# Half-position scans on one Trainium2 core: state products summed by accumulated 128x128 transposes and one transpose back, in place of identity products

## The reference

```
def step(h, inp):                       # at each of 1024 positions
    dA = jnp.exp(dtt[..., None] * A)    # 16 states a channel
    h = h * dA + (dtt * ut)[..., None] * bt[:, :, None, :]
    y = jnp.einsum('bkdn,bkn->bkd', h, ct)   # sum over the 16 states
    return (h, y)
```

## Time and profile before

| | |
|---|---|
| median of 3 runs | 6273.03 us |
| profiled execution, its own time | 6277.88 us |
| its span | 6276.1 us |
| PE (matmul) busy | 5337.5 us, 85% |
| DVE busy | 4868.2 us, 78% |
| POOL busy | 4099.8 us, 65% |
| ACT busy | 3324.5 us, 53% |
| mean granted TensorE clock | 0.937 of 2.4 GHz |

### The profile page before, as it was taken

One profiled execution on the slowest core, in us unless ns is written; L12 is line 12 of the kernel. 1 busy time (PEld: TensorE's weight loads), 2 busy tenths in 40 slices (PEclk: granted clock), 3 DMA queues, 4 the chain that ended last, 5 costly groups with the idle time before them and its releaser, 6 DMA issues. The chain is left out here.

```text
span 6276.1 us, 59374 instructions
## 1 busy us (share of the span) xinstructions
PE 5337.5 (85%) x16384; PEld 3080.8 (49%) x16384; DVE 4868.2 (78%) x5344; ACT 3324.5 (53%) x5102; POOL 4099.8 (65%) x3001
## 2 busy tenths in 40 slices
PE   6776777779999978878999988887999997888899
PEld 2222242246566544435566545443556563454777
DVE  7999769848888858866888876884888886787544
ACT  3433434347676646535667654662766674564221
POOL 6999538728788718845888853881888882685221
PEclk8989888889999989998999999998999998999999
DMA  5555224336667506525777733651776760562110
GB/s 194 211 209 209 76 105 165 114 110 234 238 239 243 189 25 227 203 82 175 242 250 237 250 107 115 214 172 44 250 249 228 256 219 31 191 214 102 53 46 33
DMA packets 339294, 1059.06 MB, mean 169 GB/s; under 512 B 31330, under 2 KB 121442, under 8 KB 333832
## 3 DMA queue, kind: packets, MB, share of 16 engines
q1 hardware_dynamic: 338952, 1055.17, 48.4%
HBM read 1046.13 MB, written 8.91 MB: 168 GB/s over the span
## 5 line engine op out<-in xcount | busy, mean ns | idle before, releaser
L849 PE MATMUL banks<-prod,ident 128*128 128x512 f32 x2640 | 1415.6, 635 | 446.7 <-DVE prod L1046 337.5
L987 POOL TENSOR_TENSOR h<-half_du_a,Bb 128x512 f32<-128x512 f32 x768 | 973.6, 1284 | 110.3 <-DMA Bb<-half_rows 57.1
L849 PEld LDWEIGHTS banks<-prod,ident 128*128 128x128 f32 x2640 | 475.4, 195 | 1041.9 <-DVE prod L1046 667.9
L933 ACT ACTIVATE banks<-half_delta_a,A 128x512 f32<-128x512 f32 x1152 | 765.4, 685 | 362.3 <-DVE prod L1046 188.7
L1033 DVE TENSOR_TENSOR_SCAN banks<-banks,h 128x512 f32<-128x512 f32 x660 | 807.4, 1223 | 134.0 <-POOL h L987 79.0
L996 POOL TENSOR_TENSOR h<-h,half_C_a 128x512 f32<-128x512 f32 x360 | 460.7, 1280 | 278.2 <-DVE half_carry_a L1038 178.0
L849 PE MATMUL banks<-h,ident 128*128 128x512 f32 x1200 | 639.3, 615 | 0.0
L1046 DVE TENSOR_TENSOR prod<-banks,half_C_a 128x512 f32<-128x512 f32 x792 | 548.1, 692 | 114.6 <-DMA half_C_a<-half_rows 16.2
L403 PE MATMUL banks<-prod,ident 128*128 128x512 f32 x648 | 375.3, 720 | 197.5 <-DVE prod L545 151.6
L873 PE MATMUL banks<-Cb,w_a 128*128 128x256 f32 x2304 | 533.8, 381 | 0.0
L1033 DVE TENSOR_TENSOR_SCAN banks<-banks,half_carry_a,h 128x512 f32<-128x512 f32 x396 | 506.3, 1279 | 32.4 <-ACT banks L933 23.8
(11 more groups left out here) (325 smaller groups left out, 10268.2 us busy)
## 6 DMA issues: line engine op xcount, KB each, us to landing
Bb<-half_rows SPq DMA_DIRECT2D x640, 512.0 KB, 4.2
Cb<-half_rows SPq DMA_DIRECT2D x320, 512.0 KB, 4.3
w_a<-w_in SPq DMA_DIRECT2D x256, 576.0 KB, 5.2
half_C_a<-half_rows SPq DMA_DIRECT2D x160, 512.0 KB, 7.3
w_b<-w_in SPq DMA_DIRECT2D x128, 576.0 KB, 5.2
Bb<-rows SPq DMA_DIRECT2D x96, 512.0 KB, 4.3
Cb<-rows SPq DMA_DIRECT2D x96, 512.0 KB, 3.7
half_C_b<-half_rows SPq DMA_DIRECT2D x80, 512.0 KB, 7.4
```

What stands on the lines that cost most here:

```text
L849: eng.matmul(ps[:, 0, :], m.ident[:, :], src, start=n == 0, stop=added(s) == (i + 1) * N, skip_group_check=True).then_inc(st.summed, 1)
L933: eng.activation(slot(s), m.delta[:, i % 2, :], ACT.Exp, scale=x.A(j, n)).then_inc(st.decay, 1)
L987: eng.tensor_tensor(m.dBu[:, s % DRIVES, :], m.du[:, i % 2, :], m.B[b % BRING][:, cols(s % 2)], ALU.mult).then_inc(st.dbu, 1)
```

## The change

Only `fused_scans` and its tensors change. A weighed state becomes the stationary operand in four blocks of 128 columns, the identity streams through with `is_transpose=True`, and the four results accumulate in bank 0: the sum over the states comes out turned in each 128x128 block. For each lane ACT then copies bank 0 to the SBUF tile `turned_sum` (`copy_sum`, at step 4 of the next lane), PE turns the four blocks back into a bank of the ring (`back`, at step 2 of PE's stream), and DVE takes from there, at step 4 in place of step 1. The ring gets a place "sum" ahead of step 6 of the next lane. A lane's first `add` waits for the copy, no longer for the take. The place of the next lane's delta is now looked for in steps 8 to 11 of every lane; before, in 4 to 7 unless a new group followed. `turned_sum` lies in the fourth half-tile of `prod`, of which the three "prods" use the others.

```diff
-    TAKE_AT, BEHIND, KEEP = 1, 2, 3
+    COPY_AT, BACK_AT, TAKE_AT, SUM_AT = 4, 2, 4, 6
+    BEHIND, KEEP = 2, 3
...
     def delta_at(i):
-        first = i * N + (8 if fresh(i + 1) else 4)
+        first = i * N + 8
...
+        if step // N and step % N == SUM_AT:
+            places.append(("sum", step // N - 1))
         places.append(("step", step))
+    places.append(("sum", LANES - 1))
...
+        elif before == "sum":
+            eng.wait_ge(st.taken, b + 1)
...
                 if n == 0 and i:
-                    eng.wait_ge(st.taken, i)
-                eng.matmul(ps[:, 0, :], m.ident[:, :], src, start=n == 0, stop=added(s) == (i + 1) * N,
-                           skip_group_check=True).then_inc(st.summed, 1)
+                    eng.wait_ge(st.copied, i)
+                for k in range(HALF // P):
+                    at = slice(k * P, (k + 1) * P)
+                    mm = eng.matmul(ps[:, 0, at], src[:, at], m.ident[:, :], start=n == 0 and k == 0,
+                                    stop=added(s) == (i + 1) * N, is_transpose=True, skip_group_check=True)
+                mm.then_inc(st.summed, 1)
+
+            def back(i):
+                eng.wait_ge(st.copied, i + 1)
+                vacated(eng, "sum", i)
+                for k in range(HALF // P):
+                    at = slice(k * P, (k + 1) * P)
+                    mm = eng.matmul(bank("sum", i)[:, at], m.turned_sum[:, at], m.ident[:, :], start=k == 0,
+                                    stop=k == HALF // P - 1, is_transpose=True, skip_group_check=True)
+                mm.then_inc(st.back, 1)
...
+                    if i and n == BACK_AT:
+                        back(i - 1)
...
+            def copy_sum(i):
+                eng.wait_ge(st.summed, (i + 1) * N)
+                if i:
+                    eng.wait_ge(st.back, i)
+                eng.activation(m.turned_sum, ps[:, 0, :], ACT.Copy).then_inc(st.copied, 1)
...
+                    if i and n == COPY_AT:
+                        copy_sum(i - 1)
...
             def take(i):
-                eng.wait_ge(st.summed, (i + 1) * N)
+                eng.wait_ge(st.back, i + 1)
...
-                x.take(eng, j, c, ps[:, 0, :]).then_inc(st.taken, 1)
+                x.take(eng, j, c, bank("sum", i)).then_inc(st.taken, 1)
```

More of the change, by code:

```diff
@@ L889, in _ @@
                         dt_product(i + 1)
+                if s == STEPS - 1:
+                    back(LANES - 1)
                 for u in up_from(s):
@@ L963, in _ @@
                         log_of(i + 1)
+                if s == STEPS - 1:
+                    copy_sum(LANES - 1)
                 for v in gelu_from(s):
@@ L1754, in build @@
                         "turned", "kept", "kept_held", "decay", "dbu", "scanned", "prod", "pooled", "summed", "taken",
-                        "hidden", "gelu", "down", "evicted", "accumulated", "sent", "reloaded", "ahead",
+                        "copied", "back", "hidden", "gelu", "down", "evicted", "accumulated", "sent", "reloaded", "ahead",
                         "w1_0", "w1_1", "w2_0", "w2_1", *(f"b{i}" for i in range(3)), *(f"c{i}" for i in range(N // 2)))
@@ L1836, in half_scan_tensors @@
                              held=m.h[:, 1:3, :].rearrange("p a (b n) -> p (a b) n", n=HALF)[:, 1:4, :],
-                             prods=m.prod[:, 0:2, :].rearrange("p a (b n) -> p (a b) n", n=HALF)[:, 0:3, :], **named)
+                             prods=m.prod[:, 0:2, :].rearrange("p a (b n) -> p (a b) n", n=HALF)[:, 0:3, :],
+                             turned_sum=m.prod[:, 1, cols(1)], **named)
             def expert_tensors(stack, name):
```

## The result

The changed kernel takes **6370.1 us** (6368.4 to 6371.9), against 6272.6 before (medians of four runs each): a ratio of 1.0153, 95% interval 1.0135 to 1.0170. I had forecast 6179 in a range of 6090 to 6300. It is slower by 98 us where I expected it faster by 94. Its span is 6367.5 us, 91 more than before.

The account below looks back on a forecast made before the run. PE, about 91% full in layer 0, was taken to bound the kernel, DVE close behind. Gains of 90 in layer 0 and 15 in layer 1, less 1, make 104, less 10 for refilling: 6273.0 - 94 = 6179 us, range 6090 to 6300.

Parts of the forecast that it names:

- What bounds the kernel: Layer 0 stage: PE as good as full, about 740 of 814 us, with DVE close behind and waiting on it.
- An add, and turning back: On PE: an add falls from 0.86 to 0.44 us; turning back costs 24 x 0.44 = 11 us a layer 0 stage.
- Rival C: On PE: transposes slower than the break-even of 0.20 us each, so the kernel slows to 6394 us; chance 0.12.
- (a) to (d): Added waits for copy, turning back, delta's product and ring place: 8 of 31 us direct waits left, 3 us on ACT added.
- 31 + 10 + 5 - 5 = 41 us: Layer 0 stage: 31 direct waits on PE, 10 of ACT's lateness, 5 echoed waits gained; 5 charged for the clock.
- wait (a): A lane's first add on PE waits for ACT's copy: even, unless ACT is in a gelu, then up to 3.5 us.
- upper bound of 30 us: Layer 0 stage: the most that the waits added by the change were thought to cost; the lower bound was 0.
- 3 x 5 us: Three layer 0 stages: gain of 5 us each that stays with 30 us of added waits, giving 6250 us.
- The end of a stage: From last weighing to take: 2.08 us becomes 2.7, so +0.6 us at each of 7 stages, 4 us.
- The clock: PE's clock in layer 0 falls from 0.99 to 0.9 to 0.94; slow bursts charged at 5 us a stage.
- rival B's far end: Transposes do not hold PE's clock up, everything at 1.2 GHz: 7570 us; chance 0.02 of this rival's 0.10.
- ACT's late decays: Layer 0 stage: an up comes 0.4 to 0.8 us sooner, so half of 20 us on ACT, 10, is gained.

Follow-up runs that it names:

- The filler run: Kernel before with only its adds as transposes, plus one ordinary fp32 product of 128x128x128 in each add; 6222.0 us, ratio 0.9919.
- the ordinary products of the same length: Kernel before with each add as two ordinary fp32 products of 128x128 blocks against 64 identity columns; 6230.1 us, ratio 0.9926.
- the chain: Copy, turning back, their waits and places; run alone as the changed kernel with identity products for adds and way back: 6466.5 us, ratio 1.0301.

## Why the prediction was wrong

**What bounds the kernel.** PE as the fullest engine of layer 0 was right, and so was that its lateness comes back to DVE. But I took DVE's waits that name PE for the price of it, and left out of the sum that PE itself stood at takes, 18 us a layer 0 stage and 13 in layer 1 with guests. The reordered kernel before shows that this was worth 20 and 9 us a stage, 80 in all.

**An add, and turning back.** Right: 0.43 to 0.44 us, one record a transpose, 103 us less busy. That a transpose has nothing to split was my reason for counting one record; the traces show the count, one against two for an identity product, and no reason for it. Rival C's break-even of 0.20 us was never near; the time fell on its side all the same, by another road.

**What is gained without the added waits.** The terms of my sum without (a) to (d), and without the end, are 31 + 10 + 5 - 5 = 41 us a layer 0 stage. The transposes alone gave 22 (814 to 792): DVE's direct waits on PE fell from 31.3 to 11.2 (1.6 on takes, 9.6 on evicts, where I expected under 5), and the 10 us of ACT's late decays didn't come. In layer 1 with guests I had counted 6 a stage; from first to last scan they are 2.6 shorter, 0.9 and 0.9 longer. So the forecast would have been too high even with the waits right.

**Waits that are added: the step that failed.** I wrote that wait (a) is "even, unless ACT is in a gelu", and left 8 us of direct waits and 3 on ACT for (a) to (d) together. The whole change costs 35 us a layer 0 stage over the transposes alone (792 to 827), and that turned the gain into a loss. PE stands 63.0 us a stage at the head of lanes where it stood 18, and the sixteen lanes without a gelu in the wait, which I had called even, have 27.3 of them. Takes alone wait 47.3 us, where I expected under 8. Every part was in the text (the gelu of 3.5 us, the guests and adds behind the add), but I priced each wait on its own against DVE's 3.1 us of slack. I did not go on to what PE must still do between the copy and the turning back: projection and half pair, 3.8 and 2.9 us, held up by the same wait and standing ahead of the turning back in PE's order. With a gelu ahead as well the take waited up to 7.9 us. My own upper bound of 30 us was too low too: it had been read off stages in which nothing on PE waited for ACT. The table of the three copy places shows the measured price. (A slip besides: the 3 x 5 us that I let stay with 30 us of added waits make 6258; the 6250 that I wrote has 8 us more of gain, which no term names.)

**The end of a stage.** 0.6 us forecast, 1.8 measured; 7 x 1.2 = 8 us missed. I had used the full clock; at all seven ends it was 0.50.

**The clock.** 0.9 to 0.94 forecast for layer 0, 0.93 measured. Bursts do meet the low clock: one of half a pair that starts at 1529.20 us takes 5.08 us at 0.55, where another takes 2.9 at 1.00. The price of 5 us a stage was not measured by itself, and the filler run leaves it open. The profiles give the clock as a share of full speed, so what the 1.2 GHz in rival B's far end stands for is a share of 0.50 throughout. No run shows that for a stage of layer 0 or of layer 1 with guests: these have 0.93 and 0.82 in the changed kernel, and 0.89 and 0.75 with the ordinary products of the same length, the run with the lowest clock of all.

**ACT's late decays.** I counted 10 us a stage from a sooner up; the transposes alone gave none (28.0 us against 26.5). In the changed kernel they did fall, to 14, as they do in all kernels with the chain. The delta's later place alone gives less than half of that, 21.8:

```profile
DVE banks L1033 <- ACT banks L933: 19.8, 17, 2.6
DVE h L1033 <- ACT banks L933: 2.0, 4, 0.8
```

What gives the rest stays open.

**Near the forecast by another road.** With the first add moved, the layer 0 window is 769 us where I expected 780 to 790, and the kernel takes 6160 us where I expected 6179. That is no proof of my sum: the same three lines give the kernel before 80 us that I hadn't counted, and on top of them the change is worth 33 us, a third of the 94.

## What to carry to other kernels

In the lane head shown above, one wait of 4.6 us at the head of PE's stream held up the projection and the half pair behind it, 3.8 and 2.9 us of work that needed nothing of what it waited for. For each added wait, list the instructions between it and the next one that another engine waits for, and move the waiting one behind those that don't need it. Here three lines of order turned a 1.5% loss into a 1.9% gain. But they also helped the kernel before by 1.2% without the change: compare in the same order, or the order's gain is put down to the change, which is worth 0.6% there.

To price such a wait, look at the waiting engine's own rows a stage, and not only at the rows of the engine behind it that name it. In four pairs of runs (the moved add in both kernels, the copy a step sooner and later) a layer 0 stage changed by 0.9 to 1.2 us for each us that PE stood less or more at bank 0. This holds for these pairs and is no rule: with the transposes alone PE stood more at takes than before, 40.5 us for 18, and the stage was 22 us shorter, since PE had less to do.

## What the runs showed of the hardware

Four float32 transposes of 128x128 take PE 0.43 to 0.44 us at a clock of 1.00, half of an identity product over 512 columns (0.86). The two-block products of 64 columns, four records as well, keep nearly the same pace; here is one add of them in the timeline at a clock of 1.00, and the guests that follow 0.45 us after it:

```profile
1607.06 0.61 PE L851 MATMUL banks<-ident,h 128*128 128x64 f32 x4
1607.51 2.81 PE L863 MATMUL banks<-big,w_a 128*128 128x256 f32 x12
```

So four records with four loads of 128 columns cost alike here, 0.43 to 0.45 us, whether a record streams 128 columns or 64. Nearly all of the clock is at one of two levels: of 4800 windows of 1 us from 1000 to 5800 us in the kernel before, 4234 show 1.00, 420 show 0.50, the rest lie between, and none is lower. In the stage without guests the clock fell from 0.84 to 0.57 with the change and the stage grew by 1 us in 361; with the transposes alone it fell to 0.53 and the stage was 3 us shorter. There, where DVE is busy 333 of 358 us, a lower clock of PE cost nothing that shows.
